# A fused attention and gated feed-forward layer: the general path's decision four steps earlier, its register load and the next batch's shift two steps earlier, the weights' conversion behind the first batch

## What is computed

```python
q = split_heads(x @ Wq.T + bq); k = ...; v = ...
scores = einsum('hbnd,hbmd->hbnm', k, q) / 16
attn = softmax(scores, axis=-1)
out = einsum('hbnm,hbmd->hbnd', attn, v)
x = layernorm(x + merge_heads(out) @ Wo.T + bo)
gate, up = x @ (w_gate / 127).T, x @ (w_up / 127).T
x = layernorm(x + (silu(gate) * up) @ (w_down / 127).T)
```

## Time and profile before

| | |
|---|---|
| median of three runs | 2596.5 us |
| the profiled execution, its own time | 2599.36 us |
| its span, first to last instruction | 2597.3 us |
| TensorE (PE) busy | 2475.1 us, 95% |
| ScalarE (ACT) busy | 2131.6 us, 82% |
| VectorE (DVE) busy | 1399.3 us, 54% |
| GpSimd (POOL) busy | 539.6 us, 21% |
| mean granted clock of TensorE | 0.987 of full speed |

### The profile page before, as it was taken

The page is one execution under the profiler, slowest core; times in us unless marked ns, Lnnn a source line. Parts: engine busy times, 40 slices in busy tenths (PEclk is TensorE's granted clock), DMA queues, the critical chain, the costliest instruction groups (busy, mean ns, idle before and its releaser), DMA issues. The chain is left out here.

```text
span 2597.3 us, 48910 instructions
## 1 busy us (share of the span) xinstructions
PE 2475.1 (95%) x18062; PEld 883.9 (34%) x18062; DVE 1399.3 (54%) x3008; ACT 2131.6 (82%) x2370; POOL 539.6 (21%) x542
## 2 busy tenths in 40 slices
PE   4878999999999999999999999999999999998996
PEld 2222243333333333333333323333333333333333
DVE  5334546464654655556464654645565465553547
ACT  1887988888898888888888898888889888887881
POOL 2101212122220312212131221212222131221113
PEclk9998999999999999999999999999999999999998
DMA  4112121030211212121030212103121120211100
GB/s 144 46 42 73 33 74 59 14 107 26 79 42 36 85 26 91 32 89 43 22 99 26 90 32 74 60 14 107 27 79 42 38 84 26 91 33 56 26 18 33
DMA packets 81750, 144.20 MB, mean 56 GB/s; under 512 B 27584, under 2 KB 29504, under 8 KB 79424
## 3 DMA queue, kind: packets, MB, share of 16 engines
q1 hardware_dynamic: 79968, 139.81, 17.2%
q10 hardware_dynamic: 1504, 0.66, 0.1%
HBM read 88.48 MB, written 50.33 MB: 53 GB/s over the span
## 5 line engine op out<-in xcount | busy, mean ns | idle before, releaser
L608 ACT ACTIVATE probs<-psum 128x1024 f32<-128x1024 f32 x2048 | 1984.3, 1024 | 366.6 <-PE psum L1046 366.4
L1046 PE MATMUL psum<-probs,v 128*32 128x512 f32 x8192 | 996.7, 604 | 0.8 <-ACT probs L608 0.8
L1046 PE MATMUL psum<-kstack,qstack 51*128 51x512 f16 x4096 | 635.2, 384 | 67.6 <-ACT probs L608 30.4
L1046 PEld LDWEIGHTS psum<-kstack,qstack 51*128 51x128 f16 x4096 | 147.0, 93 | 710.6 <-ACT probs L608 598.7
L1046 PEld LDWEIGHTS psum<-probs,v 128*32 128x32 f32 x8192 | 214.7, 109 | 489.6 <-issue 485.9
L517 POOL TENSOR_TENSOR ffn<-h,ffn 128x512 f16<-128x512 f32 x192 | 222.0, 1156 | 676.0 <-DVE ffn L793 676.0
L747 DVE SCALAR_TENSOR_TENSOR tanh_out<-tanh_out,psum 128x512 f32<-128x512 f32 x192 | 131.6, 686 | 287.1 <-ACT tanh_out L589 287.1
L510 POOL TENSOR_TENSOR rstd<-vareps,minus_half 128x2 f32<-128x2 f32 x128 | 91.1, 712 | 760.9 <-DVE vareps L815 760.9
L738 DVE SCALAR_TENSOR_TENSOR parts<-psum,scales,parts 128x512 f16<-128x512 f32 x128 | 95.3, 745 | 200.1 <-ACT parts L580 199.9
L1046 PE MATMUL psum<-ffn,gateT 128*128 128x512 f16 x768 | 199.8, 383 | 0.3 <-DVE ffn L781 0.3
L1046 PE MATMUL psum<-ffn,upT 128*128 128x512 f16 x768 | 197.7, 380 | 0.4
(11 more groups left out here) (120 smaller groups left out, 1645.1 us busy)
## 6 DMA issues: line engine op xcount, KB each, us to landing
parts_dram<-parts SPq DMA_DIRECT2D x64, 512.0 KB, 2.9
qstack<-parts_dram SPq DMA_DIRECT2D x384, 64.0 KB, 2.1
kstack<-parts_dram SPq DMA_DIRECT2D x384, 64.0 KB, 2.1
x_pre<-in_x_t SPq DMA_DIRECT2D x17, 1024.0 KB, 7.7
x_res<-in_L_attn_x SPq DMA_DIRECT2D x16, 1024.0 KB, 4.8
out<-x_res SPq DMA_DIRECT2D x32, 512.0 KB, 2.7
kstack<-shift_parts SPq DMA_DIRECT2D x384, 4.0 KB, 1.7
ffn<-in_L_ffn_w_gate SPq DMA_DIRECT2D x1, 768.0 KB, 7.0
```

The lines of the kernel that those rows point to most:

```text
L608: nc.scalar.activation(probs[:, (STEPS * b + k) % SLOTS, 2 * pr:2 * pr + 2, :], scores[pr], ACT.Exp, scale=score_scale[par]).then_inc(prob ...
L1046: return nc.tensor.matmul(o, lhsT, rhs, start=start, stop=stop)
```

## The change

Five lines are touched. The decision on VectorE is asked for at step 53 instead of 57. Both register loads, and TensorE's wait for the flag, go from step 58 to 56. The last `prepare_shift` of a batch goes from step 60 to 58 on TensorE. The constant `WIDE` is gone, and `convert_weights` is called after the whole of batch 0 in VectorE's program instead of in step 58 of it. Lines behind the removed ones move up by one or two numbers.

```diff
-DECIDE, RELOAD = 57, 58
+DECIDE, RELOAD = 53, 56
 ESC_LOAD = 58
 
-INTS, WMAX, WIDE = 24, 28, 58
+INTS, WMAX = 24, 28
@@
-PREPARES = [PER_GROUP * g + PREPARE for g in range(GROUPS - 1)] + [STEPS - 4]
+PREPARES = [PER_GROUP * g + PREPARE for g in range(GROUPS - 1)] + [STEPS - 6]
@@
                     if first and WMAX <= k < WMAX + 3:
                         find_wmax(k - WMAX)
-                    if first and k == WIDE:
-                        convert_weights()
@@
             batch(0, 0, True, False)
+            convert_weights()
             for b in range(1, BATCHES - 1, 2):
```

## The result

| | before | changed |
|---|---|---|
| median, us | 2596.55 (4 runs, 2596.32 to 2598.03) | 2560.13 (4 runs, 2558.69 to 2561.72) |
| ratio to before | | 0.9859, 95% interval 0.9842 to 0.9876 |
| profiled execution, us | 2599.36 | 2558.69 |
| its span, us | 2597.3 | 2556.6 |
| mean granted clock | 0.987 | 0.992 |

The forecast was 2559.2.

A forecast was written before the change was run, and what follows sets the result against it. TensorE, busy nearly all the time, was taken as the bound, so its idle or slow time is kernel time. Savings of 27.5 + 4.7 + 5.1 = 37.3 us off 2596.5 gave 2559.2 us, range 2553 to 2567.

The forecast's parts named there:

- Where the wait comes from: TensorE's 14 waits for line 831's flag, 26.7 us, come from the decision standing behind segment 6's transpose in VectorE's order.
- items 1 and 2: Batches 1 to 14: moving VectorE's decision costs nothing; TensorE's wait goes, 1.95 us per batch, together 27.5 us.
- Item 3: Batches 4, 9 and 14: clock lost after the stall is given back, 1.6 us three times, 4.7 us; other end none.
- Item 4: TensorE's flag load and branch, two steps earlier, 15 times each: taken as 0, at most 4.6 us for the load.
- The prediction's sign: In the changed kernel's profile, the branch records were to stay within 205 to 358 ns.
- Item 5: SyncE's six shift loads land by 2372.0, needed at worst at 2374.0: a margin of 2 us hides them.
- Batch 0's stall: Batch 0, steps 57 to 63: 5.1 us taken back from wait and slow clock, with 2.4 as the other end.
- at nothing, then: Moving the weights' conversion behind batch 0 on VectorE costs nothing; without cover TensorE would wait up to 5.0 us, once.
- a rival: Load and branch become a stall: a fetched jump at 4.35 us, fifteen times 65.3 us lost, 2624.5 us; chance 0.03.
- Batch 15's start: 2.9 us lost to slow clock over four steps without a flag wait; may go or recur, 3 us either way.
- The sum: 27.5 + 4.7 + 5.1 = 37.3 us, taken off the median of 2596.5 us, giving 2559.2 us.
- the clock is not given back: Slow stretches come as often without the stalls; only idle time returns, 29.9 us, so 2566.6 us; chance 0.07.

The follow-up runs named there:

- e1: The kernel before with only the decision moved, from step 57 to 53; 2565.44 us, ratio 0.9869.
- e2: The changed kernel with the decision back at step 57, load and wait back at 58; shift and weights stay changed; 2596.46 us, ratio 0.9989.
- e3: The kernel before with load and wait moved from step 58 to 60, the decision left at 57; 2562.78 us, ratio 0.9864.
- e10: The changed kernel with the weights' conversion back in step 58 of batch 0; 2565.08 us, ratio 0.9872.
- e9: The changed kernel run again without any edit; 2562.56 us, ratio 0.9856.
- e4: The changed kernel with the decision at step 55 instead of 53; 2569.51 us, ratio 0.9887.

## Why the prediction was right, point by point

- **Where the wait comes from, and items 1 and 2.** Right. e1, e2 and e3 show that it was the distance between decision and wait alone. 1.95 us per batch was forecast, batches are 152.05 us apart where most were 153.95: 1.9. The flag's time, 6.0 us ahead of its use, was forecast as 5.9.
- **Item 3, the clock.** Right for batches 1 to 14: no slow stretch from 220 us to the end of batch 14, in this profile or in any other without the 1.88 us stall. With item 2 it was to be 27.5 + 4.7 = 32.2 us; measured 31.8.
- **Item 4, load and branch.** Right within its bounds: 0 was taken, step 56 pays 0.04 us, 0.6 us in fourteen batches, which covers what 31.8 lacks of 32.2. The branches over the block stayed short, at a median of 323 ns. The prediction's sign, all within 205 to 358 ns, was too narrow: three of 64 took 364, 437 and 444 ns, the last two in the running stream and without idle time behind them.
- **Item 5, the shift loads.** They land by 2335.0 (issued until 2333.3, 1.7 us to land) and are needed at 2338.74. The margin was 3.7 us and not 2, mostly because their landing took 1.7 us where I had set the 3.1 of the worst.
- **Batch 0's stall.** 5.1 forecast, 5.1 found.
- **The weights' conversion, "at nothing, then".** This step failed. The cover on VectorE was as described, but the step looked only at VectorE and at TensorE's wait for the verdict. Behind the conversion stood the zero shift, behind that SyncE's two loads of 1 MB, and they hold back the far branch's fetch. Item 5 had said that SyncE is moved past, for the shift rows of a full batch; for batch 0 I didn't follow the queue beyond them. The prediction charged line 1263's 4353 ns to a rival and never asked whether it would change. With the stall gone the conversion's place is worth 5933 - 3273 ns = 2.7 us in the branch itself (e10); the whole stretch from step 63 to batch 1's step 2 is 2.9 us shorter than e10's in one profile of the changed kernel and 4.5 in the other, by the clock's luck, and the medians of e10 and e9 are 2.5 us apart. Between the two kernels it came to 1.95 us: 1.1 in the branch, the rest mostly one stretch of half clock less behind it.
- **Batch 15's start.** 3 us either way were left open, and 1.3 us came back.
- **The sum.** Terms of 37.3 us against 40.7 between the profiled executions, and 36.4 between the medians. That the median landed within 1 us of 2559.2 is partly luck: the two terms above (1.95 and 1.3) were missing, and what took about as much back in the median is probably batch 0's clock, which some executions lose in part; that is not shown, as only the profiled ones can be looked into. The rival "the clock is not given back" was wrong, and the reason against it, given for batches 1 to 14, held in every profile. Outside them it does not hold: in batch 0, where TensorE idles by ScalarE's pace, a slow stretch comes without a stall, and the prediction had named batch 15's start as the only place of such luck.

## What to carry to other kernels

Where one engine decides and another waits for it, compare the decision's place in its own queue with the wait's place in the other, in time: 14 waits of 1.9 us in a kernel at 95% busy came from one entry behind a chain that itself hung on the waiting engine. Moving either end by a few steps removes them, and leftover idleness short of that is paid at par (0.65 us each in e4). When a piece of setup is moved, follow every queue behind it down to the DMAs: the conversion itself cost TensorE nothing at either place, but the two loads that it held back cost a far jump up to 2.7 us. And when a profile is compared stretch by stretch, take the stretch long enough to hold what the clock lost before it.

## What I had not expected of the hardware

- TensorE's jump over a whole program took 3273 ns and up to 5933 ns. One packet of 16 KB on an instruction queue is in each of them, 0.9 us behind the branch, and 3.4 us behind it when loads of 2 MB were already under way; the same loads issued 0.4 us after the branch cost 0.5 us. Behind how much of the queued data the packet stands is open: in the changed kernel the DMA engines were 0.89 busy as the branch began, and it still came after 0.92 us.
- TensorE dropped to the 1.2 GHz level in batch 0 (183.43 to 186.84 us in e9, for one) without any wait longer than 1 us, in some executions of the same kernel and not in others; in the steady batches, 1.88 us of idleness did it in three of fourteen, and 0.65 us in none.
- A register load in TensorE's stream cost 0 to 0.49 us depending on the step in which it stood, though its own record is 0.3 us nearly always; why step 8 pays and steps 24 and 40 don't was not tried.
